# Latent attention: three tensor products fewer a unit, rotation partners by DMA, and a new order of the loop

## The reference

```python
q_hk   = (hidden_q @ Wq.T).reshape(B, S, 16, 128)
q_big  = einsum('bshk,hkq->bshq', q_hk, w_kc_q)          # q is 192 wide
q_big  = q_big * cos_q + rotate_half(q_big) * sin_q
kv_r   = kv_c * cos_k + rotate_half(kv_c) * sin_k        # [b, 1601, 64]
q_r    = einsum('bshq,hqr->bhsr', q_big, W_qr)           # r is 64 wide
k_r    = einsum('bld,hdr->bhlr', kv_r, W_kr)
attn   = softmax(einsum('bhsr,bhlr->bhsl', q_r, k_r))
ctx_c  = einsum('bhsl,bld->bhsd', attn, kv_r)
ctx    = einsum('bhsd,hkd->bhsk', ctx_c, w_kc_kv)
out    = ctx.reshape(B, S, 16 * 128) @ Wo.T
```

## Time and profile before

| | |
|---|---|
| median of 3 runs | 1802.81 us (1801.43 to 1810.01) |
| the profiled execution: its own time, its span | 1803.73 us, 1802.5 us |
| busy of the span | PE 93%, DVE 80%, ACT 67%, POOL 45% |
| phase e | from 729.5 us to about 1519 us |

### The profile page before, as it was taken

The page is one execution under the profiler, slowest core; times in us unless marked ns, Lnnn a source line. Parts: engine busy times, 40 slices in busy tenths (PEclk is TensorE's granted clock), DMA queues, the critical chain, the costliest instruction groups (busy, mean ns, idle before and its releaser), DMA issues.

```text
span 1802.5 us, 40836 instructions
## 1 busy us (share of the span) xinstructions
PE 1673.0 (93%) x14656; PEld 1470.0 (82%) x14656; DVE 1439.6 (80%) x3666; ACT 1200.3 (67%) x3004; POOL 810.2 (45%) x720
## 2 busy tenths in 40 slices
PE   7999998889999888899999999999999998888995
PEld 6999976658866666799999999999999997665884
DVE  5777757859856865799999999999999997786995
ACT  5766764326634543688888888888888985542663
POOL 5744422247854532444434443444444441224774
PEclk8999999879999998899999999999999999998997
DMA  5000019332339000000000000000000002402233
GB/s 176 25 1 1 1 56 362 96 99 44 52 65 280 9 2 2 23 13 13 13 12 13 30 13 13 13 13 13 13 13 1 2 2 96 197 2 86 45 52 73
DMA packets 51860, 91.61 MB, mean 51 GB/s; under 512 B 4592, under 2 KB 43632, under 8 KB 49232
## 3 DMA queue, kind: packets, MB, share of 16 engines
q1 hardware_dynamic: 42928, 78.16, 13.0%
q0 software_dynamic: 8160, 10.29, 3.6%
q10 hardware_dynamic: 576, 0.56, 0.1%
HBM read 56.13 MB, written 32.87 MB: 49 GB/s over the span
## 4 chain that ended last, share of the span: by engine, by line
PE 72%; DVE 14%; ACT 4%; issue 4%; DMA 3%; POOL 2%; SPq 0%; DVEq 0%; ACTq 0%; POOLq 0%
PE bank L100 59%; PE bank L2680 10%; DVE a_t L707 1%; DVE d_nm L1442 1%; PE bank L1938 1%; DVE a_t L704 1%; DVE d_nm L1441 1%; DMA g_sums<-g_y,g_xs 1%; DMA c_sums<-c_y,c_xs 1%; POOL c_rows L1803 1%; PE bank L1910 1%; PE bank L505 1%; PE bank L1175 1%; DVE d_lifted L1470 1%; DVE tiny L133 0%
## 5 line engine op out<-in xcount | busy, mean ns | idle before, releaser
L2780 ACT ACTIVATE e_P<-bank,e_st 128x496 f32<-128x496 f32 (+2 forms) x512 | 305.8, 599 | 32.9 <-DVE e_st L2862 32.9
L2858 DVE TENSOR_REDUCE e_st<-bank 128x1 f32<-128x496 f32 (+2 forms) x512 | 288.4, 571 | 33.7 <-PE bank L100 23.7
L2881 DVE TENSOR_TENSOR e_PT_lo<-bank,e_PT_hi 128x512 fp32r<-128x512 f32 (+1 forms) x448 | 280.9, 644 | 30.3 <-ACT e_PT_hi L2800 29.3
L2680 PE MATMUL bank<-ident,e_P 128*128 128x128 f32 (+1 forms) x1664 | 256.6, 273 | 4.0 <-DVE e_PT_lo L2881 3.9
L2800 ACT CAST e_PT_hi<-bank 128x512 fp32r<-128x512 f32 (+1 forms) x448 | 247.0, 553 | 17.7 <-PE bank L2680 10.2
L100 PE MATMUL bank<-e_PT_hi,e_kv 128*128 128x256 f32 (+1 forms) x832 | 232.1, 300 | 3.1 <-DVE e_cx_lo L2888 3.1
L100 PE MATMUL bank<-e_PT_lo,e_kv 128*128 128x256 f32 (+1 forms) x832 | 214.8, 279 | 0.0
L100 PE MATMUL bank<-e_KT,e_qk_hi 128*128 128x496 f32 (+2 forms) x512 | 207.1, 405 | 5.2 <-ACT e_P L2780 3.8
L2680 PEld LDWEIGHTS bank<-ident,e_P 128*128 128x128 f32 (+1 forms) x1664 | 197.2, 140 | 17.5 <-issue 3.1
L100 PE MATMUL bank<-e_KT,e_qk_lo 128*128 128x496 f32 (+2 forms) x512 | 177.3, 346 | 0.0
L100 PEld LDWEIGHTS bank<-e_PT_hi,e_kv 128*128 128x128 f32 (+1 forms) x832 | 156.9, 189 | 8.5 <-DVE e_cx_lo L2888 3.8
(11 more groups left out here) (493 smaller groups left out, 5281.1 us busy)
## 6 DMA issues: line engine op xcount, KB each, us to landing
c_wall<-in_c_w SPq DMA_DIRECT2D x8, 1536.0 KB, 18.9
g_wall<-in_g_w SPq DMA_DIRECT2D x8, 1536.0 KB, 19.3
c_rows<-normed SPq DMA_DIRECT2D x9, 1040.0 KB, 12.0
g_rows<-normed SPq DMA_DIRECT2D x9, 1040.0 KB, 13.5
e_stage<-in_e_w SPq DMA_DIRECT2D x16, 416.0 KB, 3.2
c_xs<-c_rows SPq DMA_DIRECT2D x23, 130.0 KB
g_xs<-g_rows SPq DMA_DIRECT2D x23, 130.0 KB
landing<-in_a_wo SPq DMA_DIRECT2D x2, 1024.0 KB, 6.1
```

The source lines that it names most:

```text
L2680: last = pe.transpose(o[0:rows, c * SEQ + i * P:c * SEQ + (i + 1) * P], p[:, i, k0:k0 + rows], ident[:])
L2780: act.activation(Pm[u % 2][:, i, STARTS[j]:STARTS[j] + n], bank[score_bank[j]][:, 0:n], ACT.Exp, bias=s[:, i, 4:5], accum_out=s[:, i, j:j ...
L2858: last = dve.tensor_reduce(s[:, i, j:j + 1], bank[score_bank[j]][:, 0:PIECES[j]], AX.X, ALU.max)
L2881: dve.tensor_tensor(lo, bank[tb_bank[at % 2]][0:rows, 0:n * SEQ].rearrange("p (c n) -> p c n", c=n), hi.bitcast(F32), ALU.subtract).then_i ...
```

## The change

The 192 query rows are no longer cut in 96 + 96 but in 128 + 64, in an order (`query_order`) in which rows and partners stand in the same chunk, in neighbouring blocks of 32 rows.

- `project_q`: the 128 rows take 6 matmuls as before. For the 64 others, `wq` holds hi and lo side by side, so that one matmul gives 64 rows with hi and 64 rows with lo: 4 matmuls instead of 6. The two half results are not added; all further steps are linear, so they go on as rows 0 to 63 and 64 to 127 of the second chunk.
- `rope_q` needs the partner rows, which now stand in another block of 32 partitions: `swap(m)` has SP bring them with 4 DMAs of 32 partitions x 2 KB, from `r0` to `r2`, when `keep_q(m)` is done. POOL multiplies `r0` with cosines meanwhile, then waits for the DMAs.
- `split_z` (POOL) replaces `upper_z` (ACT) and `lower_z` (POOL): a rounding copy of 128 x 512 and two subtractions. `repeat_z` (ACT) rounds 64 x 256 into the second half of `qr_lo`'s second chunk. `absorb_q` then takes 3 + 2 matmuls instead of 6.
- `upper_r` (ACT) has one more copy, `lower_q` and `lower_r` (DVE) two instructions instead of one; all three run once in four units.
- The second `r1` and `r2` (odd units) lie in `rows32` (the rows name it `normed`) instead of tiles of their own (`e_r`).
- At the start, SP issues the swaps of units 0 and 1 behind the context's DMAs in phase d, and POOL does `split_z(0)` and `rope_q(1)` there. The prefetch for phase f is issued by ACT at i = 32.
- The order in the loop is new on PE, ACT and DVE.

```diff
             def fetch(self, h):
 ...
+            def swap(self, m):
+                sp.wait_ge(*self.q_kept.at(m + 1))
+                for q in range(4):
+                    at, to = 32 * q, 32 * (q ^ 1)
+                    sp.dma_start(self.r2[m % 2][to:to + 32], self.r0[m % 2][at:at + 32]).then_inc(*self.q_swapped[m % 2].up(16))
...
-                for c in range(2):
-                    for d in range(DC):
-                        last = mm3(o[0:HALFQ, c * SEQ:(c + 1) * SEQ], [x[:, d, c * HALFQ:(c + 1) * HALFQ] for x in w],
-                                   (XT_hi[:, d, tok(b)], XT_lo[:, d, tok(b)]), d == 0, d == DC - 1)
+                for d in range(DC):
+                    mm3(o[:, 0:SEQ], (w[:, d, 0:P], w[:, d, 2 * P:3 * P]), (XT_hi[:, d, tok(b)], XT_lo[:, d, tok(b)]),
+                        d == 0, d == DC - 1)
+                for d in range(DC):
+                    for n, x in enumerate((XT_hi, XT_lo)):
+                        last = mm(o[:, SEQ:2 * SEQ], w[:, d, P:2 * P], x[:, d, tok(b)], d == 0 and n == 0,
+                                  d == DC - 1 and n == 1)
...
-            def upper_z(self, m):
+            def repeat_z(self, m):
                 act.wait_ge(*self.q_roped.at(m + 1))
                 if m >= 2:
                     act.wait_ge(*self.q_absorbed.at(m - 1))
-                act.copy(self.qr[m % 2][0][:], self.r1[m % 2]).then_inc(*self.z_hi.up())
+                act.copy(self.qr[m % 2][1][LAT:P, 1, :], self.r1[m % 2][0:LAT, 1, :]).then_inc(*self.z_twice.up())
...
                 pool.tensor_tensor(x1, v, self.ropeq[:, 0:2, :], ALU.mult)
-                for c in range(2):
-                    last = pool.tensor_tensor(x2[:, c, :], v[:, 1 - c, :], self.ropeq[:, 2 + c, :], ALU.mult)
-                last.then_inc(self.twice.sem, 1)
+                pool.wait_ge(*self.q_swapped[m % 2].at(64 * (m // 2 + 1)))
+                pool.tensor_tensor(x2, x2, self.ropeq[:, 2:4, :], ALU.mult).then_inc(self.twice.sem, 1)
...
-            def lower_z(self, m):
+            def split_z(self, m):
                 hi, lo = self.qr[m % 2]
+                pool.wait_ge(*self.q_roped.at(m + 1))
+                if m >= 2:
+                    pool.wait_ge(*self.q_absorbed.at(m - 1))
+                pool.tensor_copy(hi[:], self.r1[m % 2]).then_inc(*self.z_hi.up())
                 pool.wait_ge(*self.z_hi.at(m + 1))
-                pool.tensor_tensor(lo[:], self.r1[m % 2], hi[:].bitcast(F32), ALU.subtract).then_inc(*self.z_lo.up())
+                for rows, c in ((slice(0, P), 0), (slice(0, LAT), 1)):
+                    last = pool.tensor_tensor(lo[rows, c, :], self.r1[m % 2][rows, c, :], hi[rows, c, :].bitcast(F32), ALU.subtract)
+                last.then_inc(*self.z_lo.up())
...
-                        for c in range(2):
-                            last = mm3(o[:, 0:SEQ], [x[:, c, :] for x in w2[h % 2]], (z[0][:, c, :], z[1][:, c, :]),
-                                       c == 0, c == 1)
+                        mm3(o[:, 0:SEQ], (hi[:, 0, :], lo[:, 0, :]), (z[0][:, 0, :], z[1][:, 0, :]), True, False)
+                        mm(o[:, 0:SEQ], hi[:, 1, :], z[0][:, 1, :], False, False)
+                        mm(o[:, 0:SEQ], lo[:, 1, :], z[1][:, 1, :], False, True).then_inc(*q_absorbed.up())
```

More of the change, by code:

```diff
@@ L865, in decoder, with prefetch @@
         landings = {}
-        def prefetch(phase):
+        def prefetch(phase, engine=sp):
             landings[phase] = [signal(f"landed{i}") for i in range(len(LANDINGS[phase]))]
@@ L2602, in sync @@
                     sp.wait_ge(*before)
-                    for h in range(1, H):
-                        if h >= 2:
-                            sp.wait_ge(*latent.o_folded.at(h - 1))
-                        latent.fetch(h)
-                        if h == H // 2:
-                            prefetch(following)
+                    latent.fetch(1)
+                    for m in range(2, N):
+                        latent.swap(m)
+                        h, quarter = divmod(m, BATCH)
+                        if h >= 1 and quarter == 0 and h + 1 < H:
+                            sp.wait_ge(*latent.o_folded.at(h))
+                            latent.fetch(h + 1)
                 def tensor():
@@ L2724, in tensor @@
                         turn(v, 0)
+                        attend(w, 4)
                         attend(w, 5)
-                        score(u, 1, 0)
                         turn(v, 1)
                         attend(w, 6)
+                        score(u, 1, 0)
+                        project_q(a_unit(i + 2))
                         score(u, 1, 1)
-                        absorb_q(after)
+                        score(u, 1, 2)
                         turn(v, 2)
@@ L2813, in scalar @@
                             enter_scalar(0)
-                        upper_pt(v, 0)
                         upper_pt(v, 1)
                         exponential(u, 0, 2)
-                        upper_qk(after)
                         exponential(u, 0, 3)
+                        keep_context(w)
+                        if i + 2 < N:
+                            latent.keep_q(i + 2, bank[aux])
                         upper_pt(v, 2)
-                        keep_context(w)
                         if i == N:
@@ L2823, in scalar @@
                         upper_pt(v, 3)
+                        upper_qk(after)
                         exponential(u, 1, 0)
-                        if i + 2 < N:
-                            latent.keep_q(i + 2, bank[aux])
                         exponential(u, 1, 1)
```

135 lines of the change are left out of this document (74 added, 61 removed).

## The result

The changed kernel takes 1793.81 us in the median (five runs, 1791.22 to 1797.46), beside 1804.56 us for the kernel before (five runs, 1801.43 to 1810.01). The ratio is 0.9946, 95% interval 0.9931 to 0.9961: 10.7 us faster, where the forecast was 28 (1775 from 1802.81). The time lies near the upper end of the range, 1765 to 1798.

The account below looks back on a forecast made before the run. The prediction took PE to be the bound, at 12.04 us a unit. From the profiled execution, 1803.73 - 22.1 (products) - 6 (order) + 1.5 (start) - 1 (end) = 1776.1, less 0.9 for the median: 1775 us, range 1765 to 1798.

Parts of the forecast that it names:

- The products: PE in the loop: three products fewer a unit save 0.356 us, about 22.1 us, if nothing else becomes the bound.
- no other engine between: Reading of the chain that ended last: over two units PE pieces alone, 76% products and 24% transposes.
- The order: Loop order on PE, ACT, DVE: 0.1 us a unit won, 6 us in all; room laid out by hand 0.1 to 0.4.
- The DMAs: Swaps ahead of `q_roped`, for which ACT waits in `repeat_z`: called the dear part, expected under or at PE's pace.
- The ring: One unit's loop from `keep_q` through SP, landing, POOL and ACT to the next `keep_q`: 9.27 + L, 11.3 us.
- first to last of SP's issues: SP's four swap DMAs: the last issue starts 0.37 + 0.51 + 0.51 = 1.39 us behind the first.
- L: Landing time from the swap's last issue, 64 KB from SBUF to SBUF: taken as 2.0 us.
- rival 1: The ring bounds the loop, L above 2.3: unit 11.77 us, 1786 us in all; chance 0.18.
- Rival 3: Room of 0.1 to 0.4 us (banks, DVE) is missing: 0.25 us of waits a unit, 1790 us; chance 0.10.
- Rival 4: POOL's extra work stops DVE in the loop: +0.6 us a unit, 1840 us; chance 0.02.
- Rival 5: The products were not the limit: the loop keeps its pace, 1803 us; chance 0.03.
- Start and end: Units 0 and 1 start later through the swaps, +1.5 us; PE's wait for `lower_context` at the end shrinks, -1 us.

Follow-up runs that it names:

- experiment 4: Kernel before with only the new order on PE, ACT and DVE, old products, no swaps: 1795.73 us, ratio 0.9948, unit 11.93 us.
- experiment 1: Changed kernel without the swaps' DMAs, POOL's sine product reading its own rows (partner rows left out): 1772.74 us, ratio 0.9822, unit 11.59 us.
- experiment 10: New products in the old order, without the swaps' DMAs (partner rows left out): 1794.46 us, ratio 0.9950, unit 11.93 us.
- experiment 8: Changed kernel with POOL instead of ACT repeating the 64 rows, behind its low parts, all four DMAs kept: 1771.93 us, ratio 0.9809, unit 11.56 us.
- experiment 5: Changed kernel with the old order of work, new products and four DMAs kept: 1945.02 us, ratio 1.0783, unit 14.17 us.
- experiment 9: Kernel in which POOL repeats the 64 rows, put in the old order of work: 1968.75 us, ratio 1.0928, unit 14.65 us.
- experiment 3: Changed kernel with ACT's `repeat_z` moved behind the second `upper_pt` of the next iteration: 1801.75 us, ratio 0.998, unit 12.04 us.
- experiment 7: Changed kernel with two of the four swap DMAs issued by ACT behind `keep_q`, two by SP: 1852.30 us, ratio 1.0263, unit 12.93 us.

## Why the prediction was wrong

**The products: right, but not by themselves.** Five and ten matmuls start 0.12 apart, PE's busy time fell by 22.7 us, and from experiment 4 to experiment 1 the unit fell by 11.93 - 11.59 = 0.34 us (forecast 0.356), the median by 23.0 us. What the prediction did not see is that this holds in the new order only. In the old one the same edit brings 12.04 - 11.93 = 0.11 (experiment 10), because PE is held by DVE right behind `project_q`. The reading that failed here is that of the chain: "no other engine between" did not mean that PE waited for none. Order 0.11 and products 0.11 make 0.45 together, and the sum came out right since both were in the change.

**The order: right.** 0.11 against 0.1, and the slack laid out by hand held: in experiments 1 and 8 the waits view has no wait of PE for another engine. Its real worth is larger: in the old order the transfer costs 2.2 to 2.7 us a unit (experiments 5 and 9 against experiment 10).

**The DMAs: the step that failed.** "The ring is then 11.3 [...] under or at PE's pace" is wrong by 0.4, which decides, since PE's pace is 11.59 in the mean. (The upper bound named there, 11.8, was above the forecast unit of 11.58, not at it.) By its own terms, from the chain and the timelines of the changed kernel:

| term | forecast | measured |
|---|---|---|
| `keep_q` | 0.58 | 0.59 |
| first to last of SP's issues | 1.39 | 1.82 (0.55 + 0.64 + 0.63) |
| landing L | 2.0 | 2.03 |
| POOL, product and sum | 2.64 | 2.57 |
| hand-overs | 0.32 | 0.21 |
| ACT up to the next `keep_q` | 4.34 | 4.49 |
| ring | 11.27 | 11.71 |

L, on which both the range and the rivals turned, was right: 2.03 us against 2.0. The estimate by the Trainium skill (DMA: Bandwidth & Descriptors, section Anatomy of one DMA), 2.15 us, is 0.12 above it; the page gives its figures for DMAs that GpSimd issues, and these were issued by SP. The mis-sized term is the issue. It was taken from the distances of other transfers, 0.37 and 0.51; the first of these DMAs holds SP for 0.51, each further one for 0.59, and 0.04 lie between. That is 0.43 of the error of 0.44; ACT's stretch adds 0.15, and shorter hand-overs and POOL rows take it back. A sign of it stood in the earlier trace rows: the third DMA of that row holds SP for 0.59, not 0.47. Nor is it the kind of the transfer alone, for the fetch `e_stage` holds SP for 0.33 where it is issued first and for 0.58 behind a swap, in the changed kernel. So rival 1 came true, but through the issues instead of L; its time, 1786 us, holds a ring of 11.77.

**The first missing term: units that are not alike.** The prediction set the ring against a mean unit. Without a transfer the four kinds of unit take 11.58, 11.06, 11.78 and 11.93 us (experiment 1, means of 12), and a ring of 11.71 lengthens the first two and cannot be made up in the others: in the changed kernel they take 11.68, 11.73, 11.72 and 11.92 where no swap is late, 11.77 in the mean. That is 8.6 us of the 15.3 that the 48 units lost. By these numbers even the forecast ring of 11.27 would have held up the kind of unit that takes 11.06.

**The second missing term: the slowest swap of a few.** In the 48 units six swaps are late and lengthen their unit by 1.1 us on average: the other 6.7 us. All six are in units of the kind that took 11.06. The prediction priced one transfer by one number; a chain through a transfer in every unit must count how often it is late, and each time at full price where the ring has no slack. Experiment 8 has late swaps too, and they cost nothing there, inside 2.09 us of slack.

**Rival 3** (no room on the other engines) did not happen in the changed kernel, but experiments 3 and 7 show that it was near: ACT has no room between the second `upper_pt` and `keep_q`, where 0.43 us more went with 0.45 us a unit, and 1.54 with 1.35. **Rival 4** did not happen: with POOL busy for 55 us of 100 (experiment 8) PE has no gap and DVE is busy for 92.2, beside 92.5 with POOL at 51 (experiment 1). The rule of the Trainium skill (SBUF — State Buffer, section SBUF: two separate sides), by which this loop is mostly free of that conflict, agrees with these runs. **Rival 5** did in the old order, for two thirds of the products' gain. POOL's copy took 0.61, its lower bound, and all of POOL's work 5.9 us a unit (the upper end of that sum is 6.6, not 6.7).

**Start and end.** At the start, from the first `keep_q` to the loop's first `project_out`, the changed kernel takes 51.5 us and the kernel before 50.2: 1.3 longer, near the forecast 1.5. (The first `keep_q` itself starts 2.3 us earlier in the profiled execution, which was not taken apart.) At the end PE waits for `lower_context`, before and now (1430 to 1520 us):

```profile
PE bank L100 <- DVE e_cx_lo L2888: 5.8, 4, 2.7
...
PE bank L100 <- DVE e_cx_lo L2918: 3.2, 1, 3.2
```

The 1.08 us of the earlier trace rows was one of four such waits. They are 2.6 us shorter together, where the forecast counted 1. Both terms had the right sign.

## What to carry to other kernels

Lay out each ring that a transfer closes, and set it against the shortest unit of the loop, not the mean. Where it comes as near to the bound as here (11.27 forecast against 11.58), take the issue time from DMAs of the same kind in the same place of a series, or leave slack for it, since each further DMA of a swap adds its issue to the ring. Then take the waiting step out of the fullest in-order engine (here 22 us for moving one copy of 0.4 us) rather than shorten the transfer. A gain on the bounding engine counts only where the work that comes next is ready earlier too, so products and order are to be costed together.

## What had not been expected of the hardware

- SP issued these SBUF-to-SBUF DMAs of 64 KB 0.63 us apart (0.59 busy each, 0.51 the first); the DRAM-to-SBUF ones of before stood 0.37 to 0.51 apart. The same fetch held SP for 0.33 us when issued first and for 0.58 behind a swap. On ACT's queue two of the swap's DMAs took 1.42 us, on POOL's 1.03.
- In the changed kernel a swap of four DMAs was 0.7 to 1.5 us late whenever a packet of 16 KB of kind "instruction" fell inside it, and at no other time.
- PE can be held by another engine with no gap in its busy time and no other engine in its chain: in the kernel before, where both were so, `turn(v, 4)` started 0.15 us behind the end of a DVE instruction in all of 50 units.
- A rounding copy of 128x512 took POOL 0.61 us, beside 1.29 for a product of the same size with two inputs.
